# Cross-attention with 16 heads on one core: values two batches ahead, keys' stack issued a batch later, Q in four groups, the first softmax shift in halves

## What is computed

```python
B, Sq, Skv, D_MODEL, N_HEADS, D_K = 8, 112, 375, 256, 16, 16
Q = query @ Wq.T + bq          # (8, 112, 256), split in 16 heads of 16
K = key_value @ Wk.T + bk      # (8, 375, 256)
V = key_value @ Wv.T + bv
scores = Q K^T / sqrt(16)      # per batch and head: 112 x 375
attn = softmax(scores)
context = attn V               # back to (8, 112, 256)
x = context @ W_o.T + b_o + query
out = (x - mean(x)) / sqrt(var(x) + 1e-5) * gamma + beta
```

## Time and profile before

| | us |
|---|---|
| median of three runs | 157.96 (154.52 to 158.89) |
| the profiled execution | 157.02 |
| its span, first to last instruction | 155.2 |
| TensorE busy in it | 134.0 (86%) |
| VectorE busy | 105.6 (68%) |
| ScalarE busy | 80.4 (52%) |
| GpSimd busy | 60.7 (39%) |

### The profile page before, as it was taken

How to read it: one execution, slowest core, us unless ns; L and a number is a source line. 1 busy time by engine, 2 the same in 40 slices (tenths; PEclk the granted TensorE clock), 3 DMA queues, 4 the chain that set the end, 5 groups by cost and what they waited for, 6 DMA issues and landing times.

```text
span 155.2 us, 3853 instructions
## 1 busy us (share of the span) xinstructions
PE 134.0 (86%) x1466; PEld 116.7 (75%) x1466; DVE 105.6 (68%) x247; ACT 80.4 (52%) x163; POOL 60.7 (39%) x83
## 2 busy tenths in 40 slices
PE   5799989679979999889998998999899996779850
PEld 4599779468768899769988987899787875667620
DVE  6745997757937769947896699578779887031252
ACT  3648437214426666526655666465656565566410
POOL 8946997920003998404140504130023023041051
PEclk9999999987999999999999999999999999999997
DMA  4976989698950250697414050405031001001002
GB/s 128 358 259 216 269 296 227 159 270 239 301 204 2 102 156 0 169 267 235 135 52 151 4 178 4 155 2 183 24 128 34 4 4 30 4 4 30 4 0 59
DMA packets 14354, 19.58 MB, mean 126 GB/s; under 512 B 2192, under 2 KB 13520, under 8 KB 14336
## 3 DMA queue, kind: packets, MB, share of 16 engines
q1 hardware_dynamic: 13056, 17.26, 35.6%
q0 software_dynamic: 592, 1.70, 4.5%
q10 hardware_dynamic: 688, 0.38, 0.8%
HBM read 6.30 MB, written 0.92 MB: 47 GB/s over the span
## 4 chain that ended last, share of the span: by engine, by line
PE 65%; DVE 11%; DMA 10%; ACT 6%; issue 5%; SPq 1%; POOLq 0%; ACTq 0%; DVEq 0%
PE m_bank L793 19%; PE pv_bank L873 12%; PE st_bank L857 11%; PE mx_bank L834 10%; DMA q_stack<-shift 6%; DVE mx L656 6%; PE m_bank L901 4%; DMA c_raw<-ctxT 3%; PE m_bank L884 2%; ACT pw L561 2%; PE st_bank L793 2%; DMA q_stack<-q_first 1%; DVE q_hl L618 1%; PE m_bank L841 1%; ACT o_normT L552 1%
## 5 line engine op out<-in xcount | busy, mean ns | idle before, releaser
L656 DVE TENSOR_REDUCE mx<-mx_bank 112x1 f32<-112x375 f32 x128 | 64.6, 541 | 20.4 <-PE mx_bank L834 19.8
L561 ACT ACTIVATE pw<-st_bank 125x448 f32<-125x448 f32 x90 | 48.5, 548 | 48.5 <-PE st_bank L857 47.7
L834 PE MATMUL mx_bank<-k_stack,q_stack 128*112 128x376 f32 x128 | 41.3, 351 | 2.2 <-DVE mx L656 1.2
L857 PE MATMUL st_bank<-q_stack,k_stack 128*125 128x224 f32 x180 | 37.7, 294 | 1.7 <-DMA q_stack<-shift 1.7
L857 PEld LDWEIGHTS st_bank<-q_stack,k_stack 128*125 128x125 f32 x180 | 30.0, 190 | 5.5 <-issue 3.0
L834 PEld LDWEIGHTS mx_bank<-k_stack,q_stack 128*112 128x112 f32 x128 | 22.0, 181 | 4.5 <-DVE mx L656 2.4
L359 POOL TENSOR_TENSOR c_hl<-c_raw,c_hl 128x752 fp32r<-128x752 f32 x6 | 10.9, 1814 | 27.5 <-DVE c_hl L612 27.5
L873 PE MATMUL pv_bank<-pw,v_sb 125*17 125x112 f32 x720 | 20.4, 260 | 1.1 <-ACT o_raw L535 1.1
L405 POOL TENSOR_SCALAR var_eps<-mv 112x1 f32<-112x1 f32 x7 | 1.6, 223 | 49.2 <-DVE mv L692 49.2
L793 PE MATMUL m_bank<-c_hl,w_hl 128*128 128x376 f32 x84 | 18.7, 365 | 0.9 <-ACT w_hl L449 0.9
L873 PEld LDWEIGHTS pv_bank<-pw,v_sb 125*17 125x17 f32 x720 | 16.3, 97 | 3.9 <-issue 2.2
(11 more groups left out here) (102 smaller groups left out, 160.6 us busy)
## 6 DMA issues: line engine op xcount, KB each, us to landing
k_stack<-k_hl SPq DMA_DIRECT2D x48, 188.0 KB, 2.5
c_raw<-ctxT SPq DMA_DIRECT2D x8, 375.0 KB, 4.3
q_stack<-q_hl SPq DMA_DIRECT2D x6, 224.0 KB, 4.5
q_stack<-q_hl SPq DMA_DIRECT2D x6, 168.0 KB, 3.4
x_space<-x_nat POOLq DMA_DIRECT2D x1, 896.0 KB, 10.3
out<-yo SPq DMA_DIRECT2D x8, 112.0 KB, 1.9
pw<-wT SPq DMA_DIRECT2D x2, 256.0 KB, 4.8
x_space<-xT SPq DMA_DIRECT2D x1, 448.0 KB, 6.1
```

The source lines that it names most:

```text
L561: nc.scalar.activation(p_tile[0:KC, n % PR, :, :], st_of(n)[0:KC, 0:4 * Q].rearrange("p (j q) -> p j q", j=4), ACT.Exp, scale=float(DK) ** ...
L656: nc.vector.tensor_reduce(mx[b % 2][:, h % 2, q_pair(h // 2):q_pair(h // 2) + 1], mx_bank[n % MR][0:Q, 0:KV], axis=AX_X, op=ALU.max, negat ...
L834: nc.tensor.matmul(mx_bank[n % MR][0:Q, 0:KVP], q_stack[k][:, side, q_pair(h // 2), b - Q_STACKS[k][0], :], k_stack[b % 3][:, h // 2, :], ...
L857: last = nc.tensor.matmul(st_of(n)[0:KC, k * 2 * Q:(k + 1) * 2 * Q], k_stack[i % 3][:, 2 * g + k, c * KC:(c + 1) * KC], q_stack[qk][:, :, ...
```

## The change

Heads and units are renumbered over the tables below. The parts are:

- V is projected two batches ahead instead of three, in units 2, 3 and 4; so V of batch 2 moves from ahead of the loop into batch 0. K stays three ahead, in units 5 and 6 (8 and 11 in batch 0). From batch 3 on ScalarE copies K out of PSUM whole (`k_full`), makes the high part from the copy, and GpSimd subtracts for the low part; VectorE does that no more. `stack_k` of a batch is issued at the start of the following iteration of SyncE's loop, both halves together.
- Q has four groups: batch 0, batches 1 and 2, 3 to 5, 6 and 7.
- The first shift comes in halves of eight heads each. The transposition takes the maxima in one piece, and VectorE splits them afterwards from PSUM. High and low row go by a DMA each; from batch 1 on both are issued by SyncE.
- 16 heads stand ahead of the loop, and 17 instead of 16 in each batch from batch 1 on.
- `transpose_o` stands in unit 9, `transpose_o_norm` of a batch shares a bank and a place with the transposition of the maxima of a later batch (`NORM_WITH`), and `out_project` of batch i - 3 stands in unit 0 of batch i.
- The centring and scaling by the deviation moves from VectorE to GpSimd, the high part of the context from VectorE to ScalarE. GpSimd clears all of the second group's stack.
- At the end the last two `values` stand ahead of the first half's transposition.

```diff
-GB = 4
+GB = 3
...
-Q_STACKS = ((0, 1), (1, 1 + GB), (1 + GB, B))
+Q_STACKS = ((0, 1), (1, 3), (3, 6), (6, B))
...
-AHEAD = 3
-VR = AHEAD + 1
+AHEAD, V_AHEAD = 3, 2
+VR = V_AHEAD + 1
...
-U_K = (0, 2)
-U_V = (3, 5, 8)
-U_OT, U_ONT, U_OUT = 5, 9, 11
-U_BIAS = 4
-U_Q = (5, 10)
-U_NEGATE, U_MT, U_SHIFT = 5, 7, 9
-U_CONTEXT = 7
-HEADS = (1, 1, 2, 1, 2, 1, 1, 1, 2, 1, 2, 1)
...
-EARLY_HEADS = H + 4
-EARLY_JOBS = {1: ("Q", 1, 0), 3: ("Q", 1, 1), 5: ("V", 1, 0), 7: ("V", 1, 1), 9: ("V", 1, 2), 11: ("K", 2, 0),
-              13: ("K", 2, 1), 14: ("V", 2, 0), 15: ("V", 2, 1)}
-
...
+U_OUT, U_OT, U_BIAS, U_Q, U_CONTEXT = 0, 9, 0, 10, 7
+U_K = ((8, 11), (5, 6))
+U_V = (2, 3, 4)
+HALF = UNITS // 2
+NORM_WITH = {3: 0, 4: 1, 5: 2, 6: 3, 7: 5}
+U_MT = (9, 8, 8, 8, 8, 8, 8)
+
+
+EARLY_HEADS = 16
+EARLY_JOBS = {1: ("Q", 1, 0), 3: ("Q", 1, 1), 5: ("V", 1, 0), 7: ("V", 1, 1), 9: ("MT", 0, 0), 10: ("V", 1, 2),
+              13: ("K", 2, 0), 15: ("K", 2, 1)}
+FIRST_JOBS = {1: (("MT", 0, 1),), 5: (("Q", 2, 0),), 6: (("Q", 2, 1),)}
...
-FIRST_HEADS = (2, 3, 2, 3, 2)
+HEADS = (2, 1, 1, 2, 1, 2, 1, 2, 1, 1, 2, 1)
+FIRST_HEADS = ((2, 1, 2, 2, 1, 2, 2, 2, 2, 2, 1, 1),)
...
+        k_full = sb("k_full", [PART, 2, KVP])
...
                 if b >= 3:
-                    sp.wait_ge(st_full, UNITS * (b - 3) + UNITS // 2 * (t + 1))
+                    sp.wait_ge(st_full, UNITS * (b - 2))
...
+            def stack_shift(b):
+
+                k = q_stack_of(b)
+                to = q_stack[k][:, :, :, b - Q_STACKS[k][0], :].rearrange("p s a q -> p (s a) q")
+                sp.wait_ge(shift_ready, b + 2)
+                for part in range(2):
+                    row = SPREAD * (part + 1) - 1
+                    sp.dma_start(to[row:row + 1, :, :].bitcast(F32),
+                                 shift[b % 2][:, part, :].bitcast(F32)).then_inc(shift_in[b % 2], 16)
+
             for i in range(B):
-                if i >= 1 and i + AHEAD - 1 < B:
-                    stack_k(i + AHEAD - 1, 1)
+                if 1 <= i < B - V_AHEAD:
+                    for t in range(2):
+                        stack_k(i + V_AHEAD, t)
                 if i + AHEAD + 2 < B:
                     load_context(i + AHEAD + 2)
-                if i == 1:
+                if i == 4:
+                    for side in range(2):
+                        stack_q(sp, 3, side)
+                if i + 1 < B:
+                    stack_shift(i + 1)
+                if i == 0:
                     for side in range(2):
                         stack_q(sp, 2, side)
-                if i >= 2:
-                    store(i - 2)
-                if i + AHEAD < B:
-                    stack_k(i + AHEAD, 0)
-            store(B - 2)
-            store(B - 1)
+                if i >= 3:
+                    store(i - 3)
...
+                pool.wait_ge(k_hi, 2 * b + t + 1)
+                nc.gpsimd.tensor_tensor(k_hl[b % 2][:, 1, t, :], k_full[:, t, :], k_hl[b % 2][:, 0, t, :].bitcast(F32),
+                                        op=ALU.subtract).then_inc(k_lo, 1)
...
+                pool.wait_ge(rstd_ready, b + 1)
                 if b >= 2:
                     pool.wait_ge(stored[b % 2], 16 * (b // 2))
-                nc.gpsimd.tensor_tensor(yo[b % 2][:, :], z[b % 2][:, :], g_rows[:, :],
+                nc.gpsimd.tensor_scalar(yo[b % 2][:, :], z[b % 2][:, :], mv[b % 2][:, 0:1], rstd[:, 0:1],
+                                        op0=ALU.subtract, op1=ALU.mult).then_inc(y_ready, 1)
+                pool.wait_ge(y_ready, b + 1)
+                nc.gpsimd.tensor_tensor(yo[b % 2][:, :], yo[b % 2][:, :], g_rows[:, :],
                                         op=ALU.mult).then_inc(y_scaled, 1)
                 pool.wait_ge(y_scaled, b + 1)
                 nc.gpsimd.tensor_tensor(yo[b % 2][:, :], yo[b % 2][:, :], be_rows[:, :],
                                         op=ALU.add).then_inc(yo_ready, 1)
...
-            for i in range(B + 2):
-                if i >= 2:
-                    inverse_deviation(i - 2)
-                if 2 <= i < B + 1:
-                    scale_rows(i - 2)
-                if i + AHEAD + 1 < B:
+            for i in range(B - V_AHEAD):
+                if i == 0:
+                    context_lo(AHEAD + 1)
+                if i + AHEAD < B:
+                    for t in range(2):
+                        subtract_k(i + AHEAD, t)
+                if i >= 1 and i + AHEAD + 1 < B:
                     context_lo(i + AHEAD + 1)
-                if i == 0:
-                    bias_into_x()
+                if i in (1, 2):
+                    bias_into_x(i - 1)
+                if i == 2:
                     clear_q()
+                if i >= 3:
+                    inverse_deviation(i - 3)
+                    scale_rows(i - 3)
+            for b in range(B - V_AHEAD - 3, B - 1):
+                inverse_deviation(b)
+                scale_rows(b)
+            inverse_deviation(B - 1)
...
+            def take_k(b, t):
+
+                src = wait_full(act, "K", b, t)
+                if b > AHEAD:
+                    act.wait_ge(k_lo, 2 * (b - 1) + t + 1)
+                nc.scalar.activation(k_full[:, t, :], src[:, 0:KVP], ACT.Identity,
+                                     bias=bqk[:, 2 + t:3 + t]).then_inc(k_taken, 1)
+                act.wait_ge(k_taken, 2 * (b - AHEAD) + t + 1)
+                act.wait_ge(k_in[(b - 2) % 3][t], 48 * ((b - 2) // 3 + 1))
...
-                        stack_shift(i + 1)
-                    if u == (2 if i < B - 1 else 4) and i >= 1:
+                    if u == 1 and i == 0:
+                        act.wait_ge(shift_ready, 2)
+                        for part in range(2):
+                            stack_shift_half(act, 1, part)
+                    if u == (1 if i < B - 1 else 2) and i >= 1:
                         take_o(i - 1)
-                    if u - 1 in U_K and i + AHEAD < B:
-                        k_hi_part(i + AHEAD, U_K.index(u - 1))
-                    if u - 1 == U_ONT and i >= 1:
-                        take_o_norm_t(i - 1)
-                    if u - 1 in U_V[1:] and i + AHEAD < B:
-                        v_part(i + AHEAD, U_V[1:].index(u - 1))
-                    if u - 1 in U_Q and i == 0:
-                        q_hi_part(2, U_Q.index(u - 1))
+                    if i + V_AHEAD < B and u in U_V[1:]:
+                        v_part(i + V_AHEAD, u - U_V[1])
+                    if i == 0 and u in (5, 6):
+                        q_hi_part(2, u - 5)
+                    if i + AHEAD < B and u in U_K[min(i, 1)]:
+                        take_k(i + AHEAD, U_K[min(i, 1)].index(u))
+                    if u == U_CONTEXT and i + AHEAD + 1 < B:
+                        context_hi(i + AHEAD + 1)
+                    if u == U_Q and i in (1, 2):
+                        q_hi_part(3, i - 1)
+                    if i + 1 < B and u == min(U_MT[i] + 1, UNITS - 1):
+                        if i + 1 in NORM_WITH:
+                            take_o_norm_t(NORM_WITH[i + 1], "MT", i + 1)
...
+            def split_shift(src, to, n):
+
+                nc.vector.tensor_copy(to[:, 0, :], src).then_inc(shift_hi, 1)
+                dve.wait_ge(shift_hi, n)
+                nc.vector.tensor_tensor(to[:, 1, :], src, to[:, 0, :].bitcast(F32), op=ALU.subtract).then_inc(shift_ready, 1)
...
+            def transpose_max_half(t):
+                dst, full = claim("MT", 0, t)
+                pe.wait_ge(max_read, H // 2 * (t + 1))
+                nc.tensor.transpose(dst[0:NP, 0:Q], mx[0][:, :, :].rearrange("q s a -> q (s a)")[:, t:2 * NP:2],
+                                    ident[0:Q, 0:Q]).then_inc(full, 1)
+
             def transpose_max(b):
                 dst, full = claim("MT", b)
-                pe.wait_ge(neg_ready, b + 1)
-                nc.tensor.transpose(dst[0:2 * 2 * NP, 0:Q], neg_m[b % 2][:, :, :, :].rearrange("q l s a -> q (l s a)").bitcast(F32),
+                pe.wait_ge(max_read, H * (b + 1))
+                if b in NORM_WITH:
+                    norm_columns(dst, NORM_WITH[b])
+                nc.tensor.transpose(dst[0:2 * NP, D:D + Q], mx[b % 2][:, :, :].rearrange("q s a -> q (s a)"),
                                     ident[0:Q, 0:Q]).then_inc(full, 1)
...
-                if u == 0:
-                    pe.wait_ge(shift_in[i % 2], 16 * (i // 2 + 1))
+                if i == 0 and u % HALF == 0:
+                    pe.wait_ge(half_in[u // HALF], 32)
+                if i >= 1 and u == 0:
+                    pe.wait_ge(shift_in[i % 2], 32 * ((i + 1) // 2))
...
-            transpose_norm_half(0)
+                    if i + V_AHEAD < B and u in U_V:
+                        v_project(i + V_AHEAD, U_V.index(u))
+                    if i + AHEAD < B and u in U_K[min(i, 1)]:
```

More of the change, by code:

```diff
@@ L171, in build @@
         shift_in = [sem(f"shift_in{i}") for i in range(2)]
+        half_in = [sem(f"half_in{t}") for t in range(2)]
         stored = [sem(f"stored{i}") for i in range(2)]
```

(23 more changed lines are left out.)

301 lines of the change are left out of this document (151 added, 150 removed).

## The result

| | before | changed kernel |
|---|---|---|
| median of 21 runs each | 156.47 us (154.52 to 160.69) | 158.35 us (155.86 to 162.10) |
| ratio to before | | 1.0103, 95% interval 1.0066 to 1.0140 |

A ratio here compares the executions within about 1.5% of their kernel's fastest, so it can differ from the quotient of the medians. By the 2% bound this is no change, but the interval lies wholly above 1. The forecast was 154.6 us, the rivals 148, 157.6, 158.1 and 163.7; the range, 147.5 to 159.5, holds the median.

The account below looks back on a forecast made before the run. The prediction took the kernel to be bound by TensorE's own stream, so only waits could be gained; start, batches 0 to 6 and end summed to 152.8 us, plus 1.82 outside the span, 154.6 us, range 147.5 to 159.5.

Parts of the forecast that it names:

- the wait for the shift at the batch edges: Ahead of batches 1 to 7, TensorE waits for the shift's DMA, 6.8 us in all (1.2, twice 0.5, four of 1.15).
- Start: Ahead of unit 0: a first half of the shift starts 4.9 us earlier; unit 0 at 27.9 us instead of 32.88.
- Batch 0: First batch: TensorE's work plus waits for Q, banks and batch 1's shift take 17.5 us instead of 19.04.
- the shift of batch 1: At the end of batch 0: TensorE waits 1.2 us for the next batch's shift.
- rival 3: Ahead of unit 0: the low row queues behind Q's stack, unit 0 at 31 us, total 157.6 us; chance 0.10.
- Edges of batches 2 and 3: Ahead of these batches half a Q projection (0.7 us) fills the gap, leaving a shift wait of 0.5 us each.
- Edges of batches 4 to 7: Ahead of these batches a chain of 3.15 us against 2.0 of TensorE's work leaves 1.15 us of waiting each.
- Q's last group: In batch 4, heads 96 and 97 need Q's last stack, issued behind store and K: a wait of 2.0 us.
- Batches 5 and 6, end: Last windows: batch 5 without K 13.55 us, batch 6 11.55 us, the end 18.7 us.
- (1) The waits are covered: Batch edges and batch 4: waits for shift and Q's stack vanish, total about 148 us; chance 0.28.
- (2) ScalarE sets the pace: In the batches, ScalarE's added copies make TensorE wait for banks, 3.5 us more, total 158.1 us; chance 0.14.
- (4) The clock falls at edges: Waits at seven batch edges each lower TensorE's clock, 9 us more, total 163.7 us; chance 0.08.

Follow-up runs that it names:

- second profile: The changed kernel run again without an edit; the profiled execution took 157.83 us, near the median (span 156.0 us).
- first profile: The changed kernel without an edit, its longest execution: 162.10 us (span 160.2 us).
- Number 2: Changed kernel with GpSimd's load of `x_nat` issued later, behind its first K subtractions: 156.78 us, 1.0066 of the kernel before.
- number 10: Changed kernel with the two shift rows of batches 1 to 7 issued from ScalarE's queue instead of SyncE's: 167.21 us, 1.0749 of the kernel before.
- number 4: Changed kernel with Q's last stack issued an iteration earlier, ahead of the first store: 156.0 us, 1.0010 of the kernel before.
- Number 7: Changed kernel with later `x_nat` load, earlier maxima transposition, Q's last stack before the store, and shift's high row issued once ready: 149.11 us, ratio 0.9538.
- number 6: Changed kernel with later `x_nat` load, earlier maxima transposition, and Q's last stack ahead of the store: 150.54 us, 0.9607 of the kernel before.

## Why the prediction was wrong, by its steps

The step that failed is the wait for the shift at the batch edges, 6.8 us in the sum and 9.8 us measured. The mechanism, a chain at each edge that is longer than TensorE's work beside it, was right. Its sizes were not: at batch 1 the landing was taken as that of an unloaded transfer, and at batches 4 to 7 the issue was taken at half its cost. The second profile has the forecast's terms one by one; it ends at 156.0 us, the sum at 152.8.

- **Start: right.** 27.10 us, forecast 27.9; that it is 0.8 us better is within what executions differ by.
- **Batch 0: the shift of batch 1 is the step that failed first.** I put 1.2 us for it, the price of an ordinary edge. It was 2.34 in the second profile, 5.03 in the first. The prediction allows for other traffic at the start and in its rival 3, but takes an unloaded landing for this edge and never asks what is in flight at 42 us. The load of `x_nat` is, and the DMA share of the batch is 0.76. Number 2 shows the cause (0.94 us without it), number 10 that the delay can grow further with what is issued ahead. The rest of batch 0 came out as summed: 18.74, less 1.1, is 17.6 against 17.5; in it Q's wait was 0.77 where 1.2 was put, and the 1.0 for the banks that VectorE and TensorE hand to and fro was not traced apart.
- **Edges of batches 2 and 3: right.** 0.66 and 0.52 us, forecast 0.5 each. Batches 1 to 3 took 16.10, 15.15 and 15.98 us against 15.7, 14.6 and 15.65.
- **Edges of batches 4 to 7: mechanism right, size wrong.** Forecast 1.15 each; the timeline gives 1.54, 1.55, 1.50 and 1.67. The stretch ahead of batch 4:

```profile
89.50 0.26 PE L903 MATMUL m_bank<-ident,mx 112*16 112x112 f32 x1
90.03 0.25 DVE L713 CAST shift<-m_bank 16x112 fp32r<-16x112 f32 x1
90.32 0.26 DVE L715 TENSOR_TENSOR shift<-m_bank,shift 16x112 fp32r<-16x112 f32 x1
90.61 1.21 SPq L344 DMA_DIRECT2D q_stack<-shift  x2
93.07 0.48 PE L921 MATMUL st_bank<-q_stack,k_stack 128*125 128x224 f32 x2 [1.54 <-DMA q_stack<-shift]
```

  From the transposition to the unit are 3.57 us, of which 1.54 are waited: 2.03 of work, as forecast (2.0). The chain is 0.4 longer than my 3.15. I had halved SyncE's issue to 0.3 us because it is one row; two take 1.21 us, 0.6 each, as the earlier trace rows has it for 32 rows and more. The landing of 1.8 us was 0.1 under my 1.9, and VectorE's copy came 0.1 late. The prediction had the right value beside it, "with issues of 0.6 it is 1.5", and didn't take it.
- **Q's last group: right in mechanism and size.** Forecast 2.0 us in batch 4, measured 1.31 ahead of head 96 and 0.29 ahead of head 97; number 4 took 2.1 us off batch 4. The prediction looked at head 97 alone, while most of the wait stood at head 96. The store was issued 2.07 us into the batch (forecast 1.8), as soon as GpSimd was done, whose new operation cost 1.25 us and not 0.73. Q's last issue started at 9.8 (forecast 8.7) and took 2.2 us to land (forecast 2.5 to 3.4), so two errors met at 12.0, inside the 11.2 to 12.1 forecast.
- **Batches 5 and 6, end.** 14.16 and 12.29 against 13.55 and 11.55: 0.4 and 0.5 of that is the edge; the other 0.2 in each is not traced to a wait. The end, 18.39, was forecast at 18.7.

The shift waits sum to 9.8 us where I had 6.8: 1.7 of the 3.0 us are the edges of batches 4 to 7, 1.1 is that of batch 1. That 3.0 is nearly the 3.2 us between the spans, but in part by luck: the other terms cancel (start and end 1.1 and Q's two waits 0.8 under the forecast, the work of the batches over it). From the profiled 157.83 to the median are 0.5 us more. And the sign hung on little: the forecast was 2.4 us under the profiled execution of before, of which 0.5 lies above the median of 21 runs.

**Rivals.** (1) The waits are covered: not in this kernel. Number 7 has them covered, and ends at 149.1, near the 148 put for it. (2) ScalarE sets the pace: no; the only wait of a unit for the exponentials is 0.5 us in all. Its 158.1 was nearest to the median of 158.35, by luck: its mechanism had no part in it. (3) The early half isn't early: no, 27.1 us; its 157.6 was near the result by the same luck. (4) The clock falls at edges: in the two profiles it fell once inside the batches, behind the one long wait. Edges of 1.5 to 2.3 us left the clock at 1.00, so the premise of seven falls was wrong, and that of one was left out of the forecast.

The Trainium skill, "DMA: Bandwidth & Descriptors", section "Queues, rings and completion order", has a rule that bears on this: the semaphore increment of a DMA is a strongly ordered write, which lands only after every earlier write of the same DMA engine, across its queues. By it alone the two rows' few bytes could have been written early, and only their completion have waited for `x_nat`. The packets say that this is not all of it. In the first profile two of 32 left only behind the load's last one, so their bytes were late themselves, and the landing then came 1.95 us after the last packet, where 0.40 is the time without the load. The second part agrees with the rule; no run here tests it apart. The other rule of that page that the prediction weighed, that one row is spread wider than two, would have made the landing shorter than the 1.9 assumed; 1.8 was measured, so it gave next to nothing here.

## What to carry to other kernels

Before a small transfer is put on the path, list every DMA of every queue that is in flight when it starts: it may wait for the largest of them. A queue's order is also a throttle, and moving one wait to another queue can release traffic in front of it. An issue by SyncE took 0.6 us for a row of 7 KB as for a stack's 188 KB: splitting a transfer in two puts a second full issue on its chain, unless the first part goes out as soon as it is ready (number 7: shift waits of 0.4 us, 2.2 in number 6). And when one edit brings nothing, look at which wait has grown: here two edits, 1.0157 and 1.0010 alone, gave 0.9617 together. Before two profiles are compared, count from a point that both share: here the first unit alone moved by 2.5 us between executions.
